# Throwaway matmuls behind the value product of a softmax attention, in one fused transformer kernel

## The reference

```
x = x + linear_attention(layernorm(x))     # 16 heads of 8, causal running sums
x = x + experts(layernorm(x))              # 16 routed experts (top 4), 2 shared
x = x + softmax_attention(layernorm(x))    # 16 heads of 8, 256 x 256 scores a head
x = x + experts(layernorm(x))              # the same weights again
```

```
scores = einsum('bhqd,bhkd->bhqk', q, k) / sqrt(8)
attn   = softmax(scores, axis=-1)
out    = einsum('bhqk,bhkd->bhqd', attn, v)
```

## Time and profile before

| | before |
| --- | --- |
| runs, us | 559.94, 562.1, 556.33; median 559.94 |
| profiled execution, us | 560.6 (span 558.7) |
| PE busy | 518.4 us (93%), 3801 instructions |
| DVE, ACT, POOL busy | 72%, 61%, 61% |
| mean granted TensorE clock | 0.980 |
| second attention | about 262 to 395 us of the span |

### The profile page before, as it was taken

One profiled execution on the slowest core, in us unless ns is written; L12 is line 12 of the kernel. 1 busy time (PEld: TensorE's weight loads), 2 busy tenths in 40 slices (PEclk: granted clock), 3 DMA queues, 4 the chain that ended last, 5 costly groups with the idle time before them and its releaser, 6 DMA issues.

```text
span 558.7 us, 11765 instructions
## 1 busy us (share of the span) xinstructions
PE 518.4 (93%) x3801; PEld 393.0 (70%) x3801; DVE 405.0 (72%) x1093; ACT 340.2 (61%) x605; POOL 340.9 (61%) x433
## 2 busy tenths in 40 slices
PE   7888889998999999998888988989899999999996
PEld 6666566777888888886555655555678888888884
DVE  4678688586787787676777887988377686776663
ACT  3777666665556555654657677666755655555553
POOL 5888683698777877675412142141488775766663
PEclk9999899999999999999689999999999999999999
DMA  7487760652543233337423434110333453364340
GB/s 184 131 268 226 237 208 3 98 133 77 116 127 121 87 124 110 94 114 244 152 83 126 134 109 143 54 38 2 97 98 110 102 144 122 91 146 119 110 135 19
DMA packets 48549, 67.60 MB, mean 121 GB/s; under 512 B 6625, under 2 KB 18930, under 8 KB 48498
## 3 DMA queue, kind: packets, MB, share of 16 engines
q1 hardware_dynamic: 45392, 66.47, 40.8%
q10 hardware_dynamic: 3106, 0.48, 0.5%
HBM read 53.56 MB, written 13.37 MB: 120 GB/s over the span
## 4 chain that ended last, share of the span: by engine, by line
PE 65%; ACT 11%; DVE 8%; POOL 8%; issue 5%; DMA 3%; SPq 1%; POOLq 0%; ACTq 0%; DVEq 0%
PE bank L993 16%; PE bank L995 15%; PE bank L994 15%; ACT PT L877 5%; PE bank L1170 4%; PE bank L1115 4%; DVE PT L1534 2%; POOL KS L737 2%; PE bank L1147 2%; DVE MEXP L1551 2%; POOL WL L668 1%; DMA head_rows<-PHI 1%; POOL XN L617 1%; PE bank L1094 1%; PE bank L1231 1%
## 5 line engine op out<-in xcount | busy, mean ns | idle before, releaser
L737 POOL TENSOR_TENSOR KS<-PT,QS 128x512 fp32r<-128x512 f32 x144 | 185.7, 1291 | 85.9 <-ACT QS L973 80.2
L968 ACT ACTIVATE bank<-bank 128x512 f32<-128x512 f32 x128 | 74.6, 583 | 103.7 <-PE bank L995 103.2
L1648 DVE TENSOR_TENSOR PT<-CS,bank 128x512 f32<-128x512 f32 x128 | 87.7, 685 | 58.4 <-PE bank L995 56.2
L993 PE MATMUL bank<-XH,WH 128*128 128x512 f32 (+1 forms) x288 | 114.8, 399 | 0.0
L995 PE MATMUL bank<-XH,WL 128*128 128x512 f32 (+1 forms) x288 | 112.3, 390 | 0.0
L994 PE MATMUL bank<-XL,WH 128*128 128x512 f32 (+1 forms) x288 | 112.2, 390 | 0.0
L1551 DVE TENSOR_REDUCE MEXP<-bank 128x4 f32<-128x1024 f32 x64 | 78.3, 1223 | 22.7 <-PE bank L1115 22.0
L1653 DVE TENSOR_TENSOR PT<-PT,bank 128x512 f32<-128x512 f32 x128 | 88.1, 688 | 8.6 <-ACT bank L968 0.8
L973 ACT ACTIVATE QS<-PT 128x512 fp32r<-128x512 f32 x144 | 90.0, 625 | 5.7 <-DVE PT L1653 5.2
L877 ACT ACTIVATE PT<-bank 128x1024 f32<-128x1024 f32 x64 | 65.5, 1025 | 38.6 <-PE bank L1147 38.1
L1170 PE MATMUL bank<-PT,V 128*32 128x256 f32 (+1 forms) x1024 | 64.9, 373 | 0.8 <-ACT OTS L891 0.4
(11 more groups left out here) (198 smaller groups left out, 796.5 us busy)
## 6 DMA issues: line engine op xcount, KB each, us to landing
CS<-combine_rows SPq DMA_DIRECT2D x128, 256.0 KB, 3.2
head_rows<-HP SPq DMA_DIRECT2D x28, 256.0 KB, 3.0
QS<-head_rows SPq DMA_DIRECT2D x28, 256.0 KB, 2.7
KS<-head_rows SPq DMA_DIRECT2D x28, 256.0 KB, 3.2
head_rows<-PHI SPq DMA_DIRECT2D x14, 256.0 KB, 3.6
out_dram<-X SPq DMA_DIRECT2D x4, 256.0 KB, 3.6
stage<-in_L_ffn_gate_w_dram SPq DMA_DIRECT2D x5, 192.0 KB, 3.8
stage<-in_L_ffn_up_w_dram SPq DMA_DIRECT2D x5, 192.0 KB, 3.8
```

The source lines that it names most:

```text
L737: pool.tensor_tensor(GL[:, (u - 1) % 3, :], GG[:, (u - 1) % 3, :], GH[:, (u - 1) % 3, :].bitcast(f32), ALU.subtract).then_inc(F.gl, 1)
L968: act.activation(TH[:, u, :] if u < SHARED else G[u % 3][:, :], G[u % 3][:, :], ACT.Silu).then_inc(F.th, 1)
L993: pe.matmul(out, wh, vh, start=start, stop=False)
L1648: dve.tensor_tensor(ab, CS[:, e % CBUFS, :], U[u % 3][:, :], ALU.mult).then_inc(F.b, 1)
```

## The change

Behind the value product, in the second attention only, two throwaway products of the identity with itself, 128 columns wide, are added in 23 slots. In odd slots from 5 to 35 (16 of them) they write columns 256 to 383 of OT, the half that the value product of that slot doesn't use. In the even slots 8, 16, 24, 26, 28, 30 and 32 they write columns 0 to 127 of PJ, behind a wait for `A.vd`.

```
-            def keep_busy(times):
+            def keep_busy(times, bank=BANK[1][:, 0:P]):
 
                 for _ in range(times):
-                    pe.matmul(BANK[1][:, 0:P], ident[:, :], ident[:, :], start=True, stop=True)
+                    pe.matmul(bank, ident[:, :], ident[:, :], start=True, stop=True)
...
                     scores(1, n - 2)
                     scores_less_maxima(0, n - 4)
                     values_product(n - 5)
+                    if 5 <= n < UNIT_SLOT[k] and n % 2:
+                        keep_busy(2, OT[:, SEQ:SEQ + P])
+                    elif 5 < n < WEIGHTS_SLOT[k] and (g == 0 or c + 1 >= CHUNKS):
+                        pe.wait_ge(A.vd, min(c + 1, CHUNKS))
+                        keep_busy(2, PJ[:, 0:P])
                 if n == WEIGHTS_SLOT[k]:
```

## The result

| | before | after |
| --- | --- | --- |
| median, us | 559.76 (4 runs) | 566.25 (4 runs: 564.58 to 572.64) |
| ratio, 95% interval | | 1.0142 (1.0098 to 1.0185) |
| the same kernels again, 12 runs of after | 560.32 | 564.43, ratio 1.0066 (1.0040 to 1.0092) |
| profiled execution, us (span) | 560.6 (558.7) | 565.6 (563.7) |
| line 1000: instructions | 44 | 136 |

The change made the kernel slower. The forecast was 562.6 us within a range of 557 to 566: the first median lies just above the range, the second inside it.

The account below looks back on a forecast made before the run. Bound: second attention's chain alternating ScalarE's exponential and TensorE rows, line 1115 on the path, plus 17.2 us at half clock. 5.4 us lost less 1.36 covered leaves 4.1, less 1.4 from the clock: 2.7 slower, 562.6 us, range 557 to 566.

Parts of the forecast that it names:

- Price of a pair: TensorE behind the value product: two added throwaway products take 0.49 us at full clock, 0.92 us at half clock.
- On the path: Ahead of line 1115: 11 slots lose 0.23 us each, 5 tighter 0.30, slot 33 0.49, slot 5 0.92; together 5.4 us.
- The covers: Behind slots 26, 28, 29, 30, 32: lateness vanishes in waits for VectorE's or ScalarE's other work, taking back 1.36 us.
- slots 26 to 32 as long as before: Sign expected in the changed kernel's profile, second attention: these slots keep their length.
- The net loss: Second attention: 5.4 us lost on the path less 1.36 us taken back behind five slots leaves 4.1 us.
- What the clock gives back: TensorE's clock in the second attention: 1.4 us back; the first half-clock stretch stays, the second and third go.
- the two later drops: Second and third half-clock stretches, about 287.3 to 290.7 and 362.4 to 365.8 us: pairs fill idle time ahead, both go.
- The rate of 0.23 us per us: Second attention: time lost for each us at half clock; all 17.2 us lose about 4.0 us.
- The sum: Whole kernel: 4.1 - 1.4 = 2.7 us slower, 562.6 us from 559.94.
- covers gone: Rival, same 23 places: lateness doesn't vanish in VectorE's or ScalarE's other work, nothing comes back; 566.3 us, chance 0.13.
- drops anyway: Rival, second attention: the clock drops come despite the pairs and nothing is given back; 564.0 us, chance 0.20.
- a first stretch that ends sooner: Rival: pairs of slots 5 and 7 end the first half-clock stretch near 277 us; 561.4 us, chance 0.22.

Follow-up runs that it names:

- four products: Four throwaway products in place of two in the same 23 slots; ratio 1.0204 (1.0139 to 1.0270) against the kernel before, 4 runs.

## Why the prediction was wrong, step by step

**Price of a pair: wrong.** The forecast took 0.49 us from 12 old throwaways in a row, 0.12 us each. In such a row the fixed part hardly shows: it stands behind a wide row (line 1058, 128 columns, from 13.14) and pays only the change back to narrow weights, once for six products, and 6 x 0.22 = 1.32 us leaves 0.12 of the 1.44 in the earlier trace rows for that. Behind the value product a pair costs 0.64 us (1.15 at half clock), or 1.64 - 1.02 = 0.62 counted from the 1.02 us that the forecast gave the value product. With 18 exposed slots that is 18 x 0.13 to 0.15 = 2.3 to 2.7 us, the largest error. The "little for the change of weights" that the step allowed was 0.01 us; it measures 0.20.

**On the path: right.** Line 1115 was on the path. Counted row by row in the two profiles, with full-clock likes where a drop disturbed a slot, the 23 places come 8.2 us later in sum (0.36 us in each of the 11 slots, 0.44 in the 5 tighter ones, 0.62 in slot 33, 1.15 in slot 5, 0.2 in slots 11, 13 and 21 together): price less room.

**The covers: right.** Slots 26 to 33 took 387.98 - 356.18 = 31.8 us before, 0.55 of it the third drop, and 32.8 after: 1.6 us more. At 0.64 us a pair the eight slots would have lost 3 x 0.45 + 4 x 0.38 + 0.64 = 3.5 us. So covers took about 1.9 us, where 1.36 was forecast. The sign "slots 26 to 32 as long as before" did not come, and it did not fit the forecast's own sum, which let slots 27 and 31 lose.

**The net loss** was forecast at 4.1 us and measures 6.1 at the same clock. The row-by-row 8.2 us less covers of 1.9 give 6.3, so price and covers account for it.

**What the clock gives back: wrong in its way, open in its size.** 1.4 us were to come back, because the two later drops would go and none would come. The two drops did vanish, but another came, and the profile had 17.0 us at half clock after 17.2. Over 16 runs the mean is 19.3 us against 21.6, worth 0.7 us with a standard error of 0.5 (1.1 us if the runs left out of the kernel before are counted in), so neither nothing nor the forecast 1.4 us is excluded. Before the second comparison two outcomes were written down: if the pairs give nothing back, about 21 us at half clock and 1.1 to 1.3% slower; if they do, 5 us or more below the kernel before and 4 to 5 us slower. It gave 17.9 us against 22.5 beside it and 0.7%, 3.7 us, slower: nearer the second. Why the pairs gave so little is argued and not shown: they stand behind a value product that keeps TensorE running anyway, most of them filled only the 0.2 us of waiting ahead of line 1115, and the waits of 0.5 to 1.1 us at the start stayed. The rate of 0.23 us per us was the second stretch's alone; the two together give (0.8 + 0.55) / 6.8 = 0.20, and the runs show 0.29.

**The sum.** 6.1 - 0.7 = 5.4 us is what the 16 runs give, 1% of the kernel; 2.7 us was forecast. At the same clock the two comparisons agree, at 6.6 and 6.0 us, within their errors of 0.6 and 0.2; what sets them apart is 23.5 and 17.9 us at half clock. The first comparison's 1.4% lies higher partly because one of its four runs had 35 us at half clock and took 572.64 us.

**The rivals.** The second, covers gone, named 566.3 us, nearly the measured median, but by a mechanism that isn't there. The first, drops anyway, is half true: a later drop came, which is one of the signs that the forecast had named for being wrong, though four products show that filling does act. The third, a first stretch that ends sooner, did not happen in this profile: the stretch ran from about 267.6 to 277.8 us, 10.2 us as before, with the pair of slot 5 inside it at half clock. With four products in slot 5 it did.

**The two rules that the forecast weighed.** The Trainium skill (TensorE: Matmul & The Clock Gate, Back-to-back issue gap) has 81 ns a load and matmul; the traces have 0.11 us in the slope and a fixed part beside it, so the rule is further off than the row was. The Trainium skill's rule on idle gaps (the same page, Why this matters for your kernels) points at long ones; here fillers in and near waits of at most 1.1 us each took the half-clock time from 21.6 to 3.8 us a run, so in this kernel short waits matter as well.

## What to carry to other kernels

Take an instruction's price from a row with the same neighbours: here one product behind the narrow value product cost 0.42 us, and 0.22 between wide rows. In this kernel fillers paid where the engine waits and where the clock first falls, not behind work that keeps the engine running and ahead of the row that the path waits for. Where a clock varies from run to run, compare spans at the same half-clock time before believing a difference of 1%.

## What the runs showed that was not expected

Most of the spread of the kernel before is the clock: runs with 12.2 to 38.2 us at half clock took spans of 555.1 to 564.6 us. A microsecond at half clock costs 0.3 us, not the 0.5 us that half the clock would cost if the span were TensorE's work alone. And ten products in slots 2 to 5 (2, 1, 2, 3 and 2, in waits of 0.3 to 1.1 us) halve the half-clock time of the whole run, to 10.5 us.
